# Turning the blocks behind the emptying of the sums in two pairs of a batch

## The chip, the cores and the metric

One core of a Trainium2 chip runs the whole kernel. The metric is the device time of one execution in microseconds (us); less is better. The engines are named PE (matrix multiplies, with its weight loads shown apart as PEld), DVE (VectorE), ACT (ScalarE), POOL (GpSimd) and SP (which here issues the transfers).

## What is computed

The input `x` has 8 batches of 512 tokens of width 128, and two layers are applied to it. Each has an attention-like part and a feed-forward part, each on a layer-normalised input and added back to `x`. The part around the change is the first layer's attention, with 16 channels of width 64:

```python
qz_u = qz @ ternary_factor_u.T * SCALE      # [8, 512, 16 * 64]
qz_v = qz @ ternary_factor_v.T * SCALE
message_F = einsum('bcsr,bctr->bcst', qz_u, qz_v)
qh = sigmoid(message_F)
qh_v1 = einsum('bcst,bctr->bcsr', qh, qz_v)
qh_v2 = einsum('bcst,bcsr->bctr', qh, qz_u)
message_G = (qh_v1 @ ternary_factor_u + qh_v2 @ ternary_factor_v) * SCALE
```

The other parts are a mixture of 8 experts with top-64 choice (first layer), a linear attention with a hierarchical low-rank state, evaluated by running sums over tokens, and a gated feed-forward (second layer).

## The kernel before

Each engine has its own instruction stream, in an order written out by hand, and semaphores tie the streams together. After a head of some 160 us (normalisation, routing, experts, the first pair of channels), an iteration of the main part does the first layer's attention of batch i, and between its steps the second layer (`l1`) of batch i - 1. There are 8 such iterations: the first, `iteration(0, True, False)`, has no second layer in it, the other seven do; a tail does the last second layer.

Two channels are a pair, of which a batch has 8 (j from 0 to 7). A pair takes two halves of an iteration (h from 0 to 15, j = h // 2, o = h % 2), one for each of the two products `qh_v1` and `qh_v2`. On PE a half is: 4 units of scores (`scores`, each 6 products of 64 rows, three for each channel of the pair); what stands for that half in the table `MIDDLE` (the next pair's projections "pu" and "pv", the output projection "pj", steps of the second layer); then the 4 weighted sums of tokens (`weighted`, 16 matmul records) into one bank, bank 4 for o = 0 and bank 6 for o = 1. ACT turns the scores of each unit into tanh (the sigmoid in another form), L1203. A unit of `weighted` needs the tanh of its own unit and of the third unit at least.

DVE in a half does the steps of `MIDDLE` that are its own, and then `evac_o`: it empties the bank of the sums into `o_hl`, a high part (L874) and a low part (L876), when PE has finished the half's fourth weighted sum. PE's fourth unit of scores of the following half writes the same bank, so `scores` waits there, at `u % TB == 3`, for `s_oe`, which the low part raises.

In the first half of each pair (o = 0) DVE also does `turn`: it transposes the raw projections of the next pair, `raw`, in blocks of 32 by 32 into `blocks` (L799). SP waits for `s_turned` and issues 16 transfers that put the blocks in order into `tok` (`move_tokens`, L553), each with 32 KB. The first `weighted` of the next pair, two halves later, waits until all 16 have landed (`s_moved`), and so does the next `turn`, which writes `blocks` again. ACT writes the next raw projections into `raw` (L1148) after `turn` has raised `s_turned`.

The other DVE lines that are spoken of are L925 (`TENSOR_TENSOR_SCAN`, the running sum of a step "A"), L923 and L931 (the products of steps "A" and of "C" and "D"), L866 (`add_g`, the sum of the output projection) and L904 (the step "back"). On ACT, L1035 copies a step "B".

All matmuls go through one helper or another and so stand at a few lines; they are told apart by their operands. `psum<-v_parts,u_parts` are scores with o = 0 and `psum<-u_parts,v_parts` scores with o = 1. A `psum<-arena` of 128*64 is a weighted sum.

Of the kernel before, what the change touches and what calls it, by code (L numbers as in the profile page):

```python
# [117 lines left out]
PREP_K = {"pu": 1, "pv": 2}  # L118

QUARTERS = 4  # L120
MOVED = 16 * QUARTERS * QUARTERS


# [13 lines left out]
def steps_of(work):  # L137
    return work[1] if work[0] == "rows" else (work,)
# [58 lines left out]
def is_prep(work):  # L197
    return work[0] in ("pu", "pv", "pj", "sc")


def prep_index(g, k):


    return 3 + k if is_first(g) else g * 2 + 5 + k


def moved_count(i, j):

    return (i + (j > 0)) * MOVED

# [5 lines left out]
def build(nc, io):  # L216
    ctx = ExitStack()
    with ctx:
# [14 lines left out]
        def x_bank(work, second=True):  # L233
            return bank[(X_BANK if second else FIRST_X_BANK)[work]]
# [256 lines left out]
        def _(sp):  # L491
# [56 lines left out]
            def move_tokens(i, j):  # L548

                sp.wait_ge(s_turned, i * PAIRS + j)  # L550
                for r in range(QUARTERS):
                    for a in range(QUARTERS):
                        sp.dma_start(tok[32 * r:32 * r + 32, (j + 1) % 2, :, :, 32 * a:32 * a + 32].rearrange("t w k c -> t (w k) c"),  # L553
                                     blocks[32 * a:32 * a + 32].rearrange("t w (k r c) -> t (w k) r c", k=TB, r=QUARTERS)[:, :, r])\
                          .then_inc(s_moved[j], 16)
# [77 lines left out]
        def _(dve):  # L633
# [151 lines left out]
            def prep_u(g, q, par):  # L785
                dve.wait_ge(s_prep_free, prep_index(g, 1) + 1)
                if q is not None:
                    dve.wait_ge(s_f, (q - 1) * 16)
                split(u_raw, u_hl, par).then_inc(s_us, 1)

            def prep_v(g, par):
                dve.wait_ge(s_prep_free, prep_index(g, 2) + 1)
                split(v_raw, v_hl, par).then_inc(s_vs_rdy, 1)

            def turn(i, j):

                if not (isinstance(i, int) and i == 0 and j == 1):
                    dve.wait_ge(s_moved[(j - 1) % PAIRS], moved_count(i if j else i - 1, (j - 1) % PAIRS))
                nc.vector.transpose(blocks[:].rearrange("p w t -> p (w t)"), raw.rearrange("p w t -> p (w t)")).then_inc(s_turned, 1)  # L799

            def split_rows(batch):

                link(nc.vector.tensor_copy(xn1_hl[:, 0], xn1T[:, batch]))
                nc.vector.tensor_tensor(xn1_hl[:, 1], xn1T[:, batch], xn1_hl[:, 0], ALU.subtract).then_inc(s_x1, 1)
# [50 lines left out]
            def add_g(i, j):  # L855

                bk = x_bank(("pj", j), not (isinstance(i, int) and i == 0))
                dve.wait_ge(s_pj_full, i * PAIRS + j)
                if isinstance(i, int) and i == 0 and j == 2:
                    dve.wait_ge(s_pj_free, 1)  # L860
                    before = g0
                else:
                    before = gT[:]
                if isinstance(i, int) and i == 0 and j == 3:
                    dve.wait_ge(s_scf, 1)
                nc.vector.scalar_tensor_tensor(gT[:], bk[:], 0.5 * FACTOR_SCALE ** 2, before, ALU.mult, ALU.add).then_inc(s_pj_free, 1)  # L866

            def evac_o(g, j, o, some_before):

                total = sums[:, o, j % 2:j % 2 + 1]  # L870
                dve.wait_ge(s_out, g * 8 + 4 * (o + 1))
                if some_before:
                    dve.wait_ge(s_pj_full, g)
                nc.vector.tensor_scalar(o_hl[:, o, 0], o_bank[o][:], total, None, ALU.add).then_inc(s_oh, 1)  # L874
                dve.wait_ge(s_oh, g * 2 + o + 1)
                nc.vector.scalar_tensor_tensor(o_hl[:, o, 1], o_bank[o][:], total, o_hl[:, o, 0], ALU.add, ALU.subtract)\  # L876
                  .then_inc(s_oe, 1)

            def add_y(r, L):

                bk = x_bank(("y", r))
                dve.wait_ge(s_y, L * ROUNDS + r + 1)
                if r == 0:
                    ins = nc.vector.tensor_copy(y_sb[:], bk[:])
                else:
                    dve.wait_ge(s_yadd, L * ROUNDS + r)
                    ins = nc.vector.tensor_tensor(y_sb[:], bk[:], y_sb[:], ALU.add)
                ins.then_inc(s_yadd, 1)

            def l1_statistics(L):  # L890
                wait_emptied(dve, ("back", 0), L)
                link(variances(L, mv_s))
                nc.vector.tensor_scalar(ve[:], mv_s[:, :, 1], EPS, None, ALU.add).then_inc(s_stats2, 1)

            def l1_rows(L):
                dve.wait_ge(s_rstd2, L + 1)
                normalised(xn_s, L, mv_s[:, :, 0:1], rstd_s[:].unsqueeze(2)).then_inc(s_xn2, 1)
# [59 lines left out]
            def scatter_operands(i):  # L957

                dve.wait_ge(s_yl, i * 16 + 16)
                link(nc.vector.tensor_tensor(y_weighted, y_rows[:], pick_value[:, i].unsqueeze(2).broadcast_to([P, E // 2, D]), ALU.mult))  # L960
                link(nc.vector.tensor_copy(y_hl[0][:], kf32[:]))
                for e2 in range(E // 2):
                    nc.vector.tensor_scalar(selT[e2], tokens[:], pick_at[:, i, e2:e2 + 1], None, ALU.is_equal)
                nc.vector.tensor_tensor(y_hl[1][:], kf32[:], y_hl[0][:], ALU.subtract).then_inc(s_yp, 1)

            def start_g(i):
                dve.wait_ge(s_scat, i + 1)
                if isinstance(i, int):
                    dve.wait_ge(s_pj_free, 2)
                    nc.vector.memset(g0, 0.0).then_inc(s_ones, 1)  # L970
                    nc.vector.tensor_tensor(gT[:], scatter_bank(i)[:], gT[:], ALU.add).then_inc(s_scf, 1)
                else:
                    nc.vector.tensor_copy(gT[:], scatter_bank(i)[:]).then_inc(s_scf, 1)
# [5 lines left out]
            def iteration(i, attn, second):  # L979
                if not attn:  # L980
                    add_g(i, 0)
                    for step in L1_STEPS:
                        l1(step, i - 1, last_banks[STEP_AT[step] % len(last_banks)])
                        if step == ("back", 0):
                            l1_statistics(i - 1)
                            l1_rows(i - 1)
                    return
                for h in range(0 if second else FIRST_HALF, HALVES):
                    j, o = h // 2, h % 2
                    g = i * PAIRS + j  # L990
                    some_before = second or j > 1
                    if h == (0 if second else FIRST_SCATTER_HALF - 1):
                        scatter_operands(i)
                    for work in MIDDLE[h] if second else FIRST_MIDDLE[h]:
                        if work[0] == "sc":
                            start_g(i)
                        elif work[0] == "pu":
                            prep_u(g, g + 1 if some_before else None, (j + 1) % 2)
                        elif work[0] == "pv":
                            prep_v(g, (j + 1) % 2)  # L1000
                        elif work[0] == "pj":
                            add_g(i, j)
                        elif not is_prep(work) and second:
                            for step in steps_of(work):
                                l1(step, i - 1, x_bank(step))
                    if h == HALVES - 3:
                        dve.wait_ge(s_prep_full, prep_index(g, 2) + 1)
                        dve.wait_ge(s_ones, 2)
                        split_rows(i + 1)
                    if second and h == L1_AT["back", 0]:  # L1010
                        l1_statistics(i - 1)
                        l1_rows(i - 1)
                    if o == 0:
                        if not some_before:
                            for n in range(2):
                                dve.wait_ge(s_ymv[n], 16 * E)
                        turn(i, j)
                    evac_o(g, j, o, some_before)
                    for r in range(ROUNDS):
                        if second and Y_AT[r] == h:  # L1020
                            add_y(r, i - 1)

            iteration(0, True, False)

            def body(i):
# [790 lines left out]
```

## Time and profile before

| | |
|---|---|
| median of 3 runs | 1441.76 us (1440.23 to 1442.63) |
| the profiled execution, its own time | 1442.26 us |
| its span, first to last instruction | 1440.1 us |
| PE busy | 1379.7 us, 96% of the span |
| DVE busy | 897.1 us, 62% |
| ACT busy | 697.7 us, 48% |
| the core's granted TensorE clock, mean | 0.990 |
| blocks turned (L799) | 63 times, 1.23 us each |

The span is what the trace covers; some 2.2 us of the execution's time lie around it. Busy shares are averages over the whole span. Where an engine waits, the timeline and the list of waits show it beside the instruction that came after: `[0.78 <-DVE o_hl L876]` says that the engine stood idle for 0.78 us until the DVE instruction of line 876 that writes `o_hl` released it.

### The profile page before, as it was taken

To read this page: it belongs to the slowest core of one execution; us is meant where nothing else is said; L and a number is where in the kernel's file an instruction comes from. 1 tells how busy PE (TensorE), PEld (TensorE's weight loads), DVE (VectorE), ACT (ScalarE), POOL (GpSimd) and SP (SyncE) were. 2 spreads that over 40 slices of the span, in tenths; PEclk is the share of its full clock that TensorE was granted. 3 is DMA by queue.
4 is the path that set the end of the run, shared out by engine and by line. 5 is a ranking of instruction groups with operands and counts; after the bars stand their busy time and mean duration, and the time that the engine had idled before them with its cause. 6 is when DMAs were issued, how large, how long until landed. Compare 5 with 4: busy or idle time off the path is not lost.

```text
span 1440.1 us, 24389 instructions
## 1 busy us (share of the span) xinstructions
PE 1379.7 (96%) x7814; PEld 788.6 (55%) x7814; DVE 897.1 (62%) x1546; ACT 697.7 (48%) x1077; POOL 44.7 (3%) x41
## 2 busy tenths in 40 slices
PE   5989899999999999999999999999999999999977
PEld 3556554455565555555655556555555555555544
DVE  7868544556656566566556565665655665656657
ACT  6556554454444553454535545445445444454431
POOL 4000400000000000000000000000000000000000
PEclk9999999999999999999999999999999999999988
DMA  6012122222112221111222112211122211222110
GB/s 211 1 31 68 37 37 30 30 38 31 26 26 35 36 31 29 33 32 29 30 31 35 32 26 30 39 33 28 24 37 38 30 26 24 35 30 30 27 26 8
DMA packets 298256, 50.66 MB, mean 35 GB/s; under 512 B 276192, under 2 KB 296416, under 8 KB 298112
## 3 DMA queue, kind: packets, MB, share of 16 engines
q1 hardware_dynamic: 297776, 47.29, 19.4%
q8 instruction: 67, 1.10, 0.3%
q0 software_dynamic: 336, 1.64, 0.3%
q14 instruction: 77, 0.63, 0.2%
HBM read 11.64 MB, written 4.19 MB: 11 GB/s over the span
## 4 chain that ended last, share of the span: by engine, by line
issue 85%; PE 2%; DVE 1%; POOL 1%; ACT 0%; POOLq 0%; DVEq 0%
PE psum L1264 2%; DVE arena L925 0%; POOL v_w_hl L614 0%; POOL u_w_hl L614 0%; DVE arena L923 0%; DVE arena L931 0%; POOL rstd_s L629 0%; ACT arena L1035 0%; PE psum L1626 0%; DVE xn_s L669 0%; POOL u_w_hl L611 0%; POOL v_w_hl L611 0%; POOL up_hl L614 0%; DVE x_all L940 0%; POOL gate_hl L611 0%
## 5 line engine op out<-in xcount | busy, mean ns | idle before, releaser
L1203 ACT ACTIVATE arena<-psum 128x1024 f32<-128x1024 f32 x504 | 477.0, 1031 | 611.0 <-PE psum L1264 604.0
L1264 PE MATMUL psum<-arena 128*64 128x512 f32 x2016 | 462.2, 601 | 4.8 <-ACT arena L1203 4.8
L1264 PEld LDWEIGHTS psum<-arena 128*64 128x64 f32 x2016 | 133.9, 137 | 264.8 <-issue 244.3
L1264 PE MATMUL psum<-v_parts,u_parts 64*128 64x512 f32 (+1 forms) x1568 | 208.3, 402 | 12.8 <-DVE o_hl L876 12.6
L1264 PE MATMUL psum<-u_parts,v_parts 64*128 64x512 f32 x1536 | 196.3, 399 | 4.0 <-issue 3.3
L1264 PEld LDWEIGHTS psum<-v_parts,u_parts 64*128 64x128 f32 (+1 forms) x1568 | 144.1, 185 | 101.3 <-issue 58.3
L1264 PEld LDWEIGHTS psum<-u_parts,v_parts 64*128 64x128 f32 x1536 | 139.8, 184 | 84.1 <-issue 39.9
L874 DVE TENSOR_SCALAR o_hl<-psum,sums 128x512 fp32r<-128x512 f32 x126 | 93.5, 742 | 83.3 <-PE psum L1264 82.2
L876 DVE SCALAR_TENSOR_TENSOR o_hl<-psum,sums,o_hl 128x512 fp32r<-128x512 f32 x126 | 94.6, 751 | 4.5
L931 DVE TENSOR_TENSOR arena<-psum,arena 128x512 f32<-128x512 f32 x96 | 64.5, 689 | 50.4 <-PE psum L1264 48.4
L1148 ACT ACTIVATE arena<-psum 128x512 f32<-128x512 f32 x128 | 77.3, 628 | 18.3 <-PE psum L1264 18.3
L782 DVE CAST u_parts<-arena 128x512 fp32r<-128x512 f32 x64 | 28.3, 443 | 83.4 <-ACT arena L1148 83.4
L799 DVE STREAM_TRANSPOSE blocks<-arena 128x1024 f32<-128x1024 f32 x63 | 77.7, 1234 | 0.0
L923 DVE TENSOR_TENSOR arena<-psum,arena 128x512 f32<-128x512 f32 x32 | 22.1, 691 | 80.7 <-PE psum L1264 53.7
L925 DVE TENSOR_TENSOR_SCAN arena<-ones,arena 128x512 f32<-128x512 f32 x56 | 68.6, 1224 | 1.9
L1264 PE MATMUL psum<-sel_r,uT_hl 128*128 128x512 f32 x189 | 60.1, 426 | 0.0
L1264 PE MATMUL psum<-o_hl,u_w_hl 128*128 128x512 f32 x189 | 54.0, 394 | 1.7 <-DVE o_hl L876 1.7
L1264 PE MATMUL psum<-sel_r,vT_hl 128*128 128x512 f32 x189 | 54.4, 396 | 0.0
L1264 PE MATMUL psum<-o_hl,v_w_hl 128*128 128x512 f32 x189 | 53.2, 390 | 0.0
L1264 PE MATMUL psum<-arena,top_w 128*64 128x512 f32 x96 | 50.5, 608 | 1.5 <-DVE arena L931 1.5
L1264 PE MATMUL psum<-arena,bot_w 128*64 128x512 f32 x96 | 50.5, 608 | 0.0
L783 DVE TENSOR_TENSOR u_parts<-arena,u_parts 128x512 fp32r<-128x512 f32 x64 | 48.4, 756 | 2.2
(214 smaller groups left out, 1515.2 us busy)
## 6 DMA issues: line engine op xcount, KB each, us to landing
arena<-blocks SPq DMA_DIRECT2D x1008, 32.0 KB, 2.0
x_all<-in_x SPq DMA_DIRECT2D x4, 512.0 KB, 6.1
upper<-in_we SPq DMA_DIRECT2D x8, 256.0 KB, 2.7
expert_rows<-upper SPq DMA_DIRECT2D x16, 128.0 KB, 2.5
xn_s<-expert_rows SPq DMA_DIRECT2D x8, 256.0 KB, 2.9
out<-x_all SPq DMA_DIRECT2D x8, 256.0 KB, 2.8
arena<-in_e POOLq DMA_DIRECT2D x1, 896.0 KB, 6.5
arena<-in_wi POOLq DMA_DIRECT2D x1, 576.0 KB, 6.7
```

Of the source, the lines that this page charges most:

```text
L782: link(nc.vector.tensor_copy(hl[:, par, 0], raw[:]))
L783: return nc.vector.tensor_tensor(hl[:, par, 1], raw[:], hl[:, par, 0], ALU.subtract)
L799: nc.vector.transpose(blocks[:].rearrange("p w t -> p (w t)"), raw.rearrange("p w t -> p (w t)")).then_inc(s_turned, 1)
L874: nc.vector.tensor_scalar(o_hl[:, o, 0], o_bank[o][:], total, None, ALU.add).then_inc(s_oh, 1)
L876: nc.vector.scalar_tensor_tensor(o_hl[:, o, 1], o_bank[o][:], total, o_hl[:, o, 0], ALU.add, ALU.subtract)\
L923: nc.vector.tensor_tensor(ab[:], bk[:], bs_of(f)[:], ALU.mult).then_inc(s_ld, 1)
L925: link(nc.vector.tensor_tensor_scan(pre[:], ones[:], ab[:], 0.0, ALU.mult, ALU.add))
L931: nc.vector.tensor_tensor(pc[half][:, r % 2], bk[:], pre[:], ALU.mult).then_inc(s_ld, 1)
L1148: nc.scalar.activation(raw[:], bk[:], ACT.Copy, accum_out=total[:, par:par + 1]).then_inc(s_prep_free, 1)
L1203: nc.scalar.activation(th_of(un), psum[:, at:at + 2], ACT.Tanh, scale=0.5 * FACTOR_SCALE ** 2).then_inc(s_th, 2)
L1264: return nc.tensor.matmul(out, lhsT, rhs, start=start, stop=stop)
```

## The change

In the iterations that carry the second layer, for j = 0 and j = 2 (the first and the third pair, so h = 0 and h = 4), DVE does `evac_o` first and `turn` after it. For the other six pairs, and in the whole first iteration, `turn` stays in front. So of the 63 turns 14 are moved. No instruction is added or taken away.

```diff
+LATE_TURNS = (0, 2)
...
-                    if o == 0:
+                    late = second and j in LATE_TURNS
+                    if o == 0 and not late:
                         if not some_before:
                             for n in range(2):
                                 dve.wait_ge(s_ymv[n], 16 * E)
                         turn(i, j)
                     evac_o(g, j, o, some_before)
+                    if o == 0 and late:
+                        turn(i, j)
```

## Rows read from the trace of the kernel before

**Rows 1.** The page's first part: engine, busy us, share of the span, instructions.

```profile
PE 1379.7 (96%) x7814; PEld 788.6 (55%) x7814; DVE 897.1 (62%) x1546; ACT 697.7 (48%) x1077; POOL 44.7 (3%) x41
```

**Rows 2.** The waits: engine, line, releaser; us in total, times, the longest.

```profile
PE psum L1264 <- DVE o_hl L876: 14.3, 13, 3.5
```

**Rows 3.** Timeline of DVE, third pair: start us, us, engine, line, what.

```profile
644.55 1.23 DVE L799 STREAM_TRANSPOSE blocks<-arena 128x1024 f32<-128x1024 f32 x1
645.71 0.71 DVE L874 TENSOR_SCALAR o_hl<-psum,sums 128x512 fp32r<-128x512 f32 x1
646.46 0.75 DVE L876 SCALAR_TENSOR_TENSOR o_hl<-psum,sums,o_hl 128x512 fp32r<-128x512 f32 x1
650.04 0.69 DVE L923 TENSOR_TENSOR arena<-psum,bs_more 128x512 f32<-128x512 f32 x1 [2.83 <-ACT bs_more L1035]
...
652.02 0.69 DVE L931 TENSOR_TENSOR arena<-psum,arena 128x512 f32<-128x512 f32 x1
652.84 0.75 DVE L874 TENSOR_SCALAR o_hl<-psum,sums 128x512 fp32r<-128x512 f32 x1
```

**Rows 4.** Timeline of PE over the same stretch and the pair after it.

```profile
640.63 3.65 PE L1264 MATMUL psum<-arena 128*64 128x512 f32 x16
644.22 2.34 PE L1264 MATMUL psum<-v_parts,u_parts 64*128 64x512 f32 x18
647.34 0.96 PE L1264 MATMUL psum<-v_parts,u_parts 64*128 64x512 f32 x6 [0.78 <-DVE o_hl L876]
...
649.14 3.65 PE L1264 MATMUL psum<-arena 128*64 128x512 f32 x16
...
660.77 3.65 PE L1264 MATMUL psum<-arena 128*64 128x512 f32 x16
```

**Rows 5.** Timeline of ACT over the same stretch.

```profile
645.38 2.86 ACT L1203 ACTIVATE arena<-psum 128x1024 f32<-128x1024 f32 x3 [5.03 <-PE psum L1264]
648.49 1.02 ACT L1203 ACTIVATE arena<-psum 128x1024 f32<-128x1024 f32 x1 [0.26 <-PE psum L1264]
649.41 0.59 ACT L1035 ACTIVATE bs_more<-psum 128x512 f32<-128x512 f32 x1
```

**Rows 6.** First pair of batch 2, DVE and PE.

```profile
445.88 1.23 DVE L799 STREAM_TRANSPOSE blocks<-arena 128x1024 f32<-128x1024 f32 x1
447.03 0.71 DVE L874 TENSOR_SCALAR o_hl<-psum,sums 128x512 fp32r<-128x512 f32 x1
...
445.03 2.63 PE L1264 MATMUL psum<-v_parts,u_parts 64*128 64x512 f32 x18
448.58 0.98 PE L1264 MATMUL psum<-v_parts,u_parts 64*128 64x512 f32 x6 [0.92 <-DVE o_hl L876]
```

**Rows 7.** First pair of batches 4 (762, 763) and 6 (1080).

```profile
762.83 1.23 DVE L799 STREAM_TRANSPOSE blocks<-arena 128x1024 f32<-128x1024 f32 x1
764.07 0.75 DVE L874 TENSOR_SCALAR o_hl<-psum,sums 128x512 fp32r<-128x512 f32 x1
...
763.95 3.02 PE L1264 MATMUL psum<-v_parts,u_parts 64*128 64x512 f32 x24
...
1080.49 1.23 DVE L799 STREAM_TRANSPOSE blocks<-arena 128x1024 f32<-128x1024 f32 x1
...
1080.77 3.40 PE L1264 MATMUL psum<-v_parts,u_parts 64*128 64x512 f32 x24
```

**Rows 8.** DVE after the first pair's emptying, batch 3.

```profile
609.14 0.69 DVE L904 TENSOR_TENSOR x_all<-psum,x_all 128x512 f32 x1 [2.12 <-PE psum L1623]
```

**Rows 9.** The moves: SP's issues (third pair, batches 3 and 1), time to landing, PE's need.

```profile
645.82 10.43 SPq L553 DMA_DIRECT2D arena<-blocks  x16
...
328.88 11.54 SPq L553 DMA_DIRECT2D arena<-blocks  x16
...
DMA to landing us min/median/max: 1.9/2.0/3.5
...
343.74 1.51 PE L1264 MATMUL psum<-arena 128*64 128x512 f32 x6
```

## The prediction

> **What bounds the kernel now.** I began with the busy shares: PE is at work for 1379.7 of 1440.1 us [rows 1], so outside the head the time is PE's, and a change to DVE's order counts only where PE stands still for DVE. The list of waits has such an entry: PE waited for the low part of the emptied sums (L876) 13 times, 14.3 us in all [rows 2]. That is the wait for `s_oe` at a half's fourth unit of scores. I then went through PE's timeline for these 13. One is in the first iteration (3.50 us, of which the change takes nothing), one in the tail (1.73 us, the same). The other eleven are all in the two pairs that the change touches: seven in the third pair, one for each iteration with a second layer, 0.71 to 0.79 us each (5.4 together), and four in the first pair, 0.91 or 0.92 us each (3.7 together), in batches 2, 3, 5 and 7. A third pair looks like this. PE's weighted sums start at 640.63 and last 3.65, to 644.28; its next scores follow without a gap at 644.22, eighteen products, three units; the fourth unit starts only at 647.34 [rows 4]. On DVE `turn` starts at 644.55, when the sums are already complete, and the emptying follows at 645.71 and ends at 646.46 + 0.75 = 647.21 [rows 3]. DVE has no idle time in between. So the fourth unit is 0.13 us behind the end of the emptying, and 1.16 us of the wait's cause are the turn.
>
> How much PE loses I take from the length of a whole block of 24 score products: undisturbed 3.02 us [rows 7]; in the third pair 647.34 + 0.96 - 644.22 = 4.08 [rows 4], in the first pair of batch 2 448.58 + 0.98 - 445.03 = 4.53 [rows 6], in that of batch 6 3.40 [rows 7]. That is 1.06, 1.51 and 0.38 us too long. The idle figures in brackets are smaller, because they count from the modelled end of the last product.
>
> **Part 1, the emptying moved forward, third pair.** In its new place it can start at 644.55 instead of 645.71 (645.71 - 644.55 = 1.16 earlier), ends near 646.05, and an undisturbed fourth unit would start about 647.34 - 1.06 = 646.3. The wait is gone, and 1.06 us are on offer. PE can't take all of it. The half's weighted sums (649.14) need the tanh of the third unit, and ACT does three of them back to back from 645.38, to 648.24 [rows 5]; these units are scored ahead of the wait and come no earlier. 649.14 - 648.24 leaves 0.90. Behind the sums DVE is the next to be late: its product of step A (650.04) waits for ACT's copy of step B (649.41), which follows the fourth tanh (648.49, 0.26 us of idle time ahead of it) [rows 3, 5]. This chain can move up by some 0.26 to 0.30 only, and it ends in the product at 652.02, 0.69 long, right in front of the half's own emptying at 652.84. With PE 0.9 earlier that emptying would come some 0.55 us after PE's sums. In an undisturbed pair the emptying (0.75 + 0.75 behind a start 0.05 after the sums) ends 3.02 - 0.96 - 1.5 = about 0.5 us ahead of the unit that waits for it, so this lateness is just hidden. I take 0.8 us for each: 7 x 0.8 = 5.6. The bounds are 0.3, if the ACT chain sets the pace, and 1.06.
>
> **Part 2, the emptying moved forward, first pair.** In batch 2 DVE starts `turn` at 445.88, the emptying at 447.03 [rows 6]; that is 1.15 us, and the block was 1.51 too long, so all 1.15 are returned. DVE comes late by itself there (its work at the head of an iteration), so 0.36 us of the wait stay. The other three look alike: 4 x 1.15 = 4.6. In batch 6 the turn starts at 1080.49, before the sums end; the block is 0.38 too long, and I take 0.25 to 0.38, say 0.3. In batch 4 the sums' emptying starts at 764.07, on time with the turn at 762.83 in front of it [rows 7], and batch 1 is like it: nothing to gain. Together 4.9. What follows is not short of ACT here: the transposes, and eight products of the scatter lie between the scores and the weighted sums. What DVE is late with depends on how the iterations' boundaries fall; between none and all six of the iterations 2 to 7 late by the full turn, the bounds are 0 and 6 x 1.15 = 6.9.
>
> **Part 3, the turn moved back.** DVE's time is the same, 1.23 us in either place. Behind it stands DVE's next work: in the third pair L923, ahead of which DVE idles 2.83 us [rows 3], in the first pair L904, ahead of which it idles 2.12 [rows 8]. Either hides the 1.16 us that the turn now takes there: after the gain the turn ends at about 647.2 against L923 at 649.7. Without that cover it would be 1.2 us for each of 14, 17 us.
>
> The turn's end starts the 16 transfers. In a third pair it moves from 645.78 to about 647.2, by 1.45 (the length of the emptying, less their overlap). SP issues the 16 in 10.43 us, from 645.82 to 656.25; the last is issued some 0.65 before that and lands 2.0 later, at 657.6. The weighted sums that need it start at 660.77 [rows 4, 9]: 3.2 us of slack. It shrinks by 1.45 and by the 0.8 that PE comes earlier, to 0.9. In batch 1 SP takes 11.54 us from 328.88 on, the landing is at 341.8, the need at 343.74 [rows 9]: 1.95 - 2.25 = -0.3, so that one loses 0.3. In the first pairs the slack before was 2.4 to 3.9 by the same reckoning; the turn moves by 1.45 where DVE was late and by 2.7 (764.07 + 1.5 against 762.83) where it was not, and 0 to 1.2 us are left. I take 0.3 for pair three of batch 1 and nothing else. The bounds: nothing at all, or, if SP needs 11.54 everywhere, 0.3 more in each of about ten, 3 us.
>
> Here a rule speaks against the change. The landing takes 2.0 us from issue, in every place [rows 9], and the gap between landing and need is what the later turn uses up. The Trainium skill, "DMA: Bandwidth & Descriptors", Rules for kernel authors, says to issue a DMA early and wait on its semaphore late, so that its fixed setup cost overlaps; the change issues 14 x 16 of them later. By that rule alone the sum would be a loss where the slack is used up; the rows say that it is not quite.
>
> **Sum.** 5.6 + 4.9 - 0.3 = 10.2 us, against the profiled execution's own 1442.26: 1432.1. The median of the runs shown is 0.5 below that execution, so I put the median of the new kernel at 1431.7.
>
> **Rivals.**
> - *Only the first pairs pay.* In the third pair, ACT's fourth tanh and DVE's products hold the pace, and each yields 0.3: 4.9 + 2.1 - 0.3 = 6.7, so 1435. For it speaks that ACT has only 0.26 us idle there; against it, that DVE's own lateness is covered by 0.5 us. Chance 0.13.
> - *No change.* The time that PE wins is given back before the iteration ends, at its boundary or at steps whose releaser does not move. Speaks for it: PE waits for ACT in many small places. Against: the waits with a fixed time are none; each chain starts from PE's own products. 1441.8, give or take 1. Chance 0.07.
> - *The moves come late.* This is the one on the other side. If the 16 transfers need longer when issued later, PE's weighted sums of the second and fourth pair wait. The gain is 10.5 over 14 places, 0.75 us for each, so it decides when the mean wait passes 0.75, that is when landing comes some 1.5 us later than reckoned. With the longest landing seen (3.5 against 2.0) and the slower issue (11.54 against 10.43) it is 2.6 later, less 0.9 of slack, 1.7 for each: 14 x 1.7 - 10.5 = 13 us slower, 1455. Both are rare in the trace. Chance 0.04.
> - *The first pairs are late by another pattern.* With none late the gain is 5.3 (1436.5), with six late 5.3 + 6.9 = 12.2 (1429.5). This is part of the forecast's own range.
>
> **Numbers.** The forecast has a chance of 0.76, with 1429.5 to 1434.5 as its own range. With the rival of the first pairs, the range is 1429 to 1436.5. A difference below 0.2% (2.9 us) can hardly be told from no change here. Faster by more than that: 0.88; within it: 0.08; slower: 0.04.
>
> **What would show it.** The waits of PE for L876 fall from 13 to some 6, and from 14.3 to about 6.5 us: the two outside, and the rest of 0.3 us in the late first pairs. A third pair's scores block is about 3.0 to 3.2 us long instead of 4.08. In the first and third pair L799 stands behind L876. The first `weighted` of the second and fourth pair shows no wait for the moves but in batch 1. The forecast is wrong if PE's gap reappears in front of weighted sums, if DVE's L874 in the half after the third pair is late by more than 0.5 us, or if the first pairs' lateness is gone or everywhere.

## The result and the profile after

The changed kernel takes 1432.2 us in the median of 4 runs (1431.69 to 1434.59), the kernel before 1441.91 us beside it. The ratio is 0.9938 with a 95% interval from 0.9922 to 0.9954: faster by 0.6%, 9.7 us, against a forecast of 1431.7. Two later measurements of the same kernel gave 1435.25 and 1435.73 us (below), 6.2 and 6.5 us less than before by their ratios; the first ratio makes it 8.9. So the gain is somewhere from 6 to 9 us, and the 0.5 us between forecast and first result say little. The profiled execution is the slowest of the 4: 1434.59 us, its span 1432.6.

The page's first part and three rows of the waits, after:

```profile
PE 1374.9 (96%) x7814; PEld 787.8 (55%) x7814; DVE 897.0 (63%) x1546; ACT 696.6 (49%) x1077; POOL 44.7 (3%) x41
```

```profile
PEld psum L1270 <- DVE o_hl L879: 7.5, 11, 4.0
PE psum L1270 <- DVE o_hl L879: 5.2, 2, 3.5
PEld psum L1270 <- DMA arena<-blocks: 4.8, 7, 1.1
```

L1270, L879, L877, L802 and L926 are the L1264, L876, L874, L799 and L923 of before; L1209 and L1041 on ACT are its L1203 and L1035. PE's wait for the emptied sums went from 14.3 us, 13 times [rows 2] to 5.2 us, twice: only the two outside the change are left. The weight loads (PEld) still wait for L879 eleven times. The longest, 4.0 us, is the one in the first iteration; the others are of 0.22 or 0.45 us and cost PE little: in the first pairs of batches 3, 5 and 7 the block of 24 score products takes 3.29 to 3.33 us, where an undisturbed one takes 3.02. A wait that was not there has come instead: seven times for the moved blocks.

The third pair of batch 3, DVE and PE (start, us; compare [rows 3, 4]):

```profile
642.54 0.74 DVE L877 TENSOR_SCALAR o_hl<-psum,sums 128x512 fp32r<-128x512 f32 x1
643.31 0.75 DVE L879 SCALAR_TENSOR_TENSOR o_hl<-psum,sums,o_hl 128x512 fp32r<-128x512 f32 x1
643.98 1.23 DVE L802 STREAM_TRANSPOSE blocks<-arena 128x1024 f32<-128x1024 f32 x1
647.65 0.69 DVE L926 TENSOR_TENSOR arena<-psum,bs_more 128x512 f32<-128x512 f32 x1 [2.44 <-ACT bs_more L1041]
```

```profile
638.62 3.65 PE L1270 MATMUL psum<-arena 128*64 128x512 f32 x16
...
642.20 3.04 PE L1270 MATMUL psum<-v_parts,u_parts 64*128 64x512 f32 x24
...
646.27 3.65 PE L1270 MATMUL psum<-arena 128*64 128x512 f32 x16
...
656.43 0.86 PE L1270 MATMUL psum<-o_hl,u_w_hl 128*128 128x512 f32 x3
657.12 0.84 PE L1270 MATMUL psum<-o_hl,v_w_hl 128*128 128x512 f32 x3
658.14 3.65 PE L1270 MATMUL psum<-arena 128*64 128x512 f32 x16 [0.17 <-DMA arena<-blocks]
```

The 24 score products are one unbroken block of 3.04 us (4.08 before). From one start of weighted sums to the next it is 646.27 - 638.62 = 7.65 us, where it was 649.14 - 640.63 = 8.51: 0.86 gained. From there to the fourth pair's sums it is 658.14 - 646.27 = 11.87, where it was 660.77 - 649.14 = 11.63: 0.24 given back, at the wait for the blocks.

These intervals, taken for all halves of all seven batches from the starts of PE's weighted sums, are the account that the rest goes by (us, sum over the seven batches, against the profiled execution of before):

| kernel | first pair, half 0 to 1 | half 1 to 2 | third pair, half 4 to 5 | half 5 to 6 |
|---|---|---|---|---|
| the change | -4.50 | 0.00 | -5.91 | +2.44 |
| the change, second measurement | -3.75 | +0.26 | -5.93 | +3.66 |
| the change, third measurement | -4.66 | +0.04 | -5.92 | +2.71 |

All other halves together differ by less than 0.3 us, but for the step from one iteration to the next (+0.5 in the first two rows, +2.4 in the third, of which 2.26 us in one batch). The stretches that the change does not touch differ as well: the head and the first iteration together by +1.0, -1.6 and 0.0 us in the three rows, the time after the last half by -1.0, -1.3 and -1.3. So a difference of 1 or 2 us between two whole times says nothing about a half, and the halves are compared one by one.

What held up the blocks? SP issues them as before, in 10.43 us, and a usual landing would be 1.4 us after the end of that, at 657.1:

```profile
645.24 10.43 SPq L556 DMA_DIRECT2D arena<-blocks  x16
```

PE, and so the blocks, were ready only at 658.14. The transfers by queue, in the stretch from 655.7 to 658.1 us (packets, MB, share of the 16 DMA engines):

```profile
q1 hardware_dynamic: 529, 0.06, 20.6%
q8 instruction: 1, 0.02, 2.4%
```

One packet loads instructions. Its share of 2.4% of 16 engines over 2.4 us is 0.92 us on one of them: the reading is that it stands in front of the last blocks' packets there. (The trace does not name the engine of a packet, so this much is inferred, from a landing that comes 1.0 us late.) The Trainium skill, "Runtime: NRT & Kernel Launch", Instruction fetch mechanics, says that an engine's sequencer fetches its instructions ahead by DMA, 256 at a time in blocks of 16 KiB, and that this is mostly hidden. The trace agrees with the size (0.02 MB). In the kernel before, the stretch from 656.3 to the landing at 657.6 shows queue q1 alone:

```profile
q1 hardware_dynamic: 516, 0.06, 36.2%
```

There the load came later, behind the landing. In the trace after such a packet meets the end of the third pair's moves in six of seven batches, all but batch 1, and these six are the ones that lose: 0.23 to 0.77 us each, batch 1 only 0.03.

### The profile page after: what moved, and what is told of

It reads as the page before. It is cut to its first block, busy times and chain, and to the rows that moved or that the text cites. A ratio compares the mean times of both kernels' runs of the same rounds, so it can differ in the third digit from the quotient of the medians.

```text
span 1432.6 us, 24389 instructions
## 1 busy us (share of the span) xinstructions
PE 1374.9 (96%) x7814; PEld 787.8 (55%) x7814; DVE 897.0 (63%) x1546; ACT 696.6 (49%) x1077; POOL 44.7 (3%) x41
## 4 chain that ended last, share of the span: by engine, by line
issue 86%; DVE 2%; POOL 1%; PE 1%; ACT 0%; POOLq 0%; DVEq 0%
PE psum L1270 1%; DVE arena L928 1%; DVE arena L926 0%; DVE arena L934 0%; POOL v_w_hl L617 0%; POOL u_w_hl L617 0%; POOL rstd_s L632 0%; DVE arena L950 0%; ACT arena L1041 0%; PE psum L1632 0%; DVE xn_s L672 0%; POOL u_w_hl L614 0%; POOL v_w_hl L614 0%; POOL up_hl L617 0%; DVE x_all L943 0%
## 5 line engine op out<-in xcount | busy, mean ns | idle before, releaser
L1209 ACT ACTIVATE arena<-psum 128x1024 f32<-128x1024 f32 x504 | 475.7, 1031 | 604.7 <-PE psum L1270 597.8
L1270 PE MATMUL psum<-arena 128*64 128x512 f32 x2016 | 462.4, 601 | 7.6 <-ACT arena L1209 4.8
L1270 PEld LDWEIGHTS psum<-arena 128*64 128x64 f32 x2016 | 134.0, 137 | 268.5 <-issue 241.3
L1270 PE MATMUL psum<-v_parts,u_parts 64*128 64x512 f32 (+1 forms) x1568 | 205.0, 401 | 4.2 <-DVE o_hl L879 3.5
L1270 PE MATMUL psum<-u_parts,v_parts 64*128 64x512 f32 x1536 | 196.4, 399 | 4.6 <-issue 3.9
L1270 PEld LDWEIGHTS psum<-v_parts,u_parts 64*128 64x128 f32 (+1 forms) x1568 | 145.0, 185 | 88.6 <-issue 51.1
L1270 PEld LDWEIGHTS psum<-u_parts,v_parts 64*128 64x128 f32 x1536 | 139.3, 184 | 85.2 <-issue 45.3
L877 DVE TENSOR_SCALAR o_hl<-psum,sums 128x512 fp32r<-128x512 f32 x126 | 93.8, 745 | 88.4 <-PE psum L1270 88.2
L879 DVE SCALAR_TENSOR_TENSOR o_hl<-psum,sums,o_hl 128x512 fp32r<-128x512 f32 x126 | 94.6, 751 | 4.4
L802 DVE STREAM_TRANSPOSE blocks<-arena 128x1024 f32<-128x1024 f32 x63 | 77.7, 1234 | 0.0
L926 DVE TENSOR_TENSOR arena<-psum,arena 128x512 f32<-128x512 f32 x32 | 22.1, 690 | 80.2 <-PE psum L1270 53.4
L1270 PE MATMUL psum<-sel_r,uT_hl 128*128 128x512 f32 x189 | 60.1, 426 | 0.0
L1270 PE MATMUL psum<-o_hl,u_w_hl 128*128 128x512 f32 x189 | 54.0, 394 | 1.7 <-DVE o_hl L879 1.7
L1270 PE MATMUL psum<-sel_r,vT_hl 128*128 128x512 f32 x189 | 54.5, 396 | 0.0
L1270 PE MATMUL psum<-o_hl,v_w_hl 128*128 128x512 f32 x189 | 53.2, 390 | 0.0
L1270 PE MATMUL psum<-arena,top_w 128*64 128x512 f32 x96 | 49.3, 595 | 1.5 <-DVE arena L934 1.5
L1270 PE MATMUL psum<-arena,bot_w 128*64 128x512 f32 x96 | 49.3, 595 | 0.0
```

Source lines behind the costliest of these rows:

```text
L926: nc.vector.tensor_tensor(ab[:], bk[:], bs_of(f)[:], ALU.mult).then_inc(s_ld, 1)
L1209: nc.scalar.activation(th_of(un), psum[:, at:at + 2], ACT.Tanh, scale=0.5 * FACTOR_SCALE ** 2).then_inc(s_th, 2)
L1270: return nc.tensor.matmul(out, lhsT, rhs, start=start, stop=stop)
```

## The experiments

**The changed kernel again, and three edits of it.** The three were made to tell two readings of the new wait apart: the load of instructions (theory 1), or blocks that are simply too late (theory 2).

> The changed kernel itself, beside the three others of this call. All theories: 1432 us, 0.993 of the kernel before. Its trace should again show PE waiting for the moved blocks in front of the weighted sums of the fourth pair (half 6) in all seven batches, 0.2 to 0.7 us each, some 2.4 us in all.

1435.25 us (1434.4 to 1435.87, 5 runs), ratio 0.9957 [0.9944, 0.9971]. The wait is there in all seven batches, but it costs more, 3.66 us. The time expected was missed by 3 us. The two profiled executions are alike in time, 1434.40 us for this one and 1434.59 for the first, but not in their parts. The wait for the blocks is 1.2 us longer in this one and the first pairs gain 0.75 less; against that, 3.0 us less are spent where the change does nothing: 1.6 in the head, 1.0 in the first iteration and 0.4 after the last half.

> The changed kernel with 32 small products in PE's stream at its very beginning, where PE waits for the first rows anyway. They compute nothing that is used; they shift all later instructions of PE by some 128. Theory 1 (instruction loads at fixed places of PE's stream meet the last moves of the third pair): the loads fall some 10 us elsewhere, the landing of the third pair's moves comes 1.4 us after SP's last issue instead of 2.4, the waits ahead of half 6 go: 2 us less, about 1430 us, unless the loads now meet the moves of the first pair. Theory 2 (simply too late): nothing changes, 1432 us.

```diff
             pe.wait_ge(s_first, 16 * len(first_consts))
+            for _ in range(32):
+                mm(bank[7][:, 0:4], ident[:], ident[:, 0:4])
```

1440.68 us (11 runs), ratio 0.9991 [0.9982, 1.0]. The products were not free: they waited for a load and then took 13.8 us, which made the head some 7 us longer. Behind the head the expectation of theory 1 holds: half 5 to 6 costs 0.56 us instead of 2.44 to 3.66. Of these, 0.41 are in batch 1, where a load of instructions now meets the end of the moves, and the six batches that it has left lose at most 0.07 each: the loss goes where the packet goes.

> The changed kernel with 8 of the third pair's 16 moves issued by POOL, the other 8 by SP, in the seven late batches; POOL waits for the turn as SP does. Both theories: the moves land 2 us or more earlier if POOL issues one in under 1 us, the waits ahead of half 6 go, and the third pair keeps all of its 0.86 us: 2.4 us less, about 1429.8 us. If POOL needs much more than 1 us for each, it is slower than the changed kernel: 8 x 1.5 = 12 us from the turn on would land after the need and cost some 0.5 us in each batch.

```diff
+            with pool.Fori(0, B - 1) as n:
+                rstd_rows(n)
+                pool.wait_ge(s_turned, n * PAIRS + PAIRS + 2)
+                pool.tensor_tensor(pool_idle[:], powc[:], powc[:], ALU.add)
+                for r in range(QUARTERS // 2, QUARTERS):
+                    for a in range(QUARTERS):
+                        move_block(pool, 2, r, a, s_moved_pool)
+            rstd_rows(B - 1)
...
-                for r in range(QUARTERS):
+                for r in range(QUARTERS // 2 if j == 2 and not (isinstance(i, int) and i == 0) else QUARTERS):
```

1430.68 us (1429.33 to 1431.45), ratio 0.9922 [0.9908, 0.9936]: 4.6 us less than the changed kernel beside it, where 2.4 was expected. POOL and SP issue side by side (batch 3):

```profile
644.27 4.66 POOL L503 DMA_DIRECT2D arena<-blocks  x8
```

```profile
644.08 5.20 SPq L503 DMA_DIRECT2D arena<-blocks  x8
```

Both are done 5 us sooner, so that one packet of 0.92 us can't hold them up until the need, and half 5 to 6 is back at -0.06 us. It keeps the whole gain of the third pair and gives nothing back. Not all of the 4.6 us are the moves: 2.4 to 3.7 are the wait for them, and another 1.3 us stand in the halves from 6 on, in each batch alike. Those the kernel with two queues and all turns in front has too (below), and what they come from is not shown.

> The changed kernel with add_g (L869, 0.68 us) of the first and third pair put behind the turn: DVE empties the sums, turns, adds. The turn, and with it the 16 moves, ends about 0.6 us earlier where DVE was late. Theory 1 (the last transfers of the third pair stand behind a transfer of 16 KB that loads instructions, which comes at a place of PE's stream): the moves that meet it land when it is done, so the waits of the fourth pair stay, and only the 0.3 us that is left of the wait for the sums in the late first pairs comes back, four times: 1431 us. Theory 2 (the moves are simply too late by 0.2 to 0.7 us, because they begin 1.45 us later): the waits go, 2.4 + 1.2 us less, 1428.5 us.

```diff
-                            add_g(i, j)
+                            if not (second and j in LATE_TURNS):
+                                add_g(i, j)
...
                     if o == 0 and late:
                         turn(i, j)
+                        add_g(i, j)
```

1477.95 us (1476.16 to 1480.79), ratio 1.0257 [1.0243, 1.0271]. Neither theory had this. PE, in the first pair of batch 3, and the waits:

```profile
613.58 0.96 PE L1272 MATMUL psum<-v_parts,u_parts 64*128 64x512 f32 x6
617.04 3.70 PE L1272 MATMUL psum<-v_parts,u_parts 64*128 64x512 f32 x18 [2.50 <-DVE arena L869]
```

```profile
PEld psum L1272 <- DVE arena L869: 36.0, 14, 3.0
```

`add_g` empties a bank too. In the first pair it is bank 2, and the next half's second unit of scores writes it, two units sooner than the bank of the sums is written; in the third pair it is bank 6, which the third unit writes, one unit sooner. Put behind the emptying and the turn it makes the seven first pairs 24.6 us longer than in the kernel before and the third ones 13.4, by the same account. Only part of that is PE standing still, 30.0 us in 14 waits against some 48 us that the two pairs lose to the changed kernel. Much of the rest is the clock: behind the stand of 2.50 us above, the granted clock is 0.57 in the mean from 617.04 to 620.50, near its lower level (1.2 GHz), and 18 score products take 3.70 us instead of 2.34 [rows 4]. The trace has 11 stretches at the lower level in the seven batches, 41 us in all; the changed kernel's trace has none there. The run says nothing about the theories. But the changed kernel has this wait once: in batch 2 of its first profile PE stands 0.64 us for L869, since DVE is late as a whole there, and that first pair gains 0.53 instead of 1.15 us.

**One pair at a time, and the shift again, hidden.**

> Only the first pair's turn is put behind the emptying (LATE_TURNS = (0,)). By the account of the changed kernel's trace the first pairs give 4.5 us and lose next to nothing to late moves: 1437.3 us against 1441.8. If the gain of the first pairs depended on the third, it would be nearer to 1441.

> Only the third pair's turn is put behind the emptying (LATE_TURNS = (2,)). By the account it gains 0.86 us seven times, 5.9 us, gives 2.4 to 3.6 us back in front of the fourth pair's weighted sums, where the moves land late, and wins 0.2 elsewhere: 1438.2 to 1439.4 us. The sum of this gain and of that of the other run should be the whole gain, 6.5 to 9.7 us. If the moves did not cost anything, it would be 1435.9.

`LATE_TURNS = (0,)`: 1435.36 us, ratio 0.9965 [0.9952, 0.9979], 6.0 us less than before. `LATE_TURNS = (2,)`: 1438.14 us, ratio 0.9974 [0.9964, 0.9985], 3.2 us less. Their accounts are those of the change, each for its own pair: -4.73 in the first pairs and nothing in half 4 to 6; -5.92 in the third pairs and +2.87 behind them, -0.09 in the first. The parts add up (6.0 + 3.2 = 9.2, where the whole gave 6 to 9), and half by half one does not depend on the other; the times alone are too coarse to show it (the nine runs of the second spread over 6.3 us). So the third pair's turn, which takes more off PE's wait, earns less.

> The changed kernel with 22 small products of ones in PE's stream at its very beginning, ahead of the loads, where PE waits 11 us for the first rows; nothing reads their result. They shift PE's later instructions by some 88. Theory 1 (a load of instructions at fixed places of PE's stream meets the last moves of the third pair): the loads come some 7 us earlier in each half 5, the last moves land 1.4 us after SP's last issue, the waits ahead of half 6 shrink from 0.2 to 0.9 us each to 0.1 or less: 2.4 to 3.5 us less than the changed kernel on the same chip (1432 to 1435), so 1429.5 to 1432. Theory 2 (the moves are too late by themselves): no change.

```diff
+            pe.wait_ge(s_ones, 1)
+            for _ in range(22):
+                mm(bank[7][:, 0:4], ones[:, 0:P], ones[:, 0:4])
             pe.wait_ge(s_first, 16 * len(first_consts))
```

1431.6 us (1430.51 to 1434.23), ratio 0.9936 [0.9923, 0.995]. Half 5 to 6 costs 0.10 us instead of 2.44 to 3.66, with the turn exactly as late as in the change. Batch 3, SP's issues, PE, and the transfers from 653.9 to 655.6 us:

```profile
643.06 10.81 SPq L556 DMA_DIRECT2D arena<-blocks  x16
```

```profile
644.08 1.51 PE L1270 MATMUL psum<-arena 128*64 128x512 f32 x6
...
655.71 3.65 PE L1270 MATMUL psum<-arena 128*64 128x512 f32 x16
```

```profile
q1 hardware_dynamic: 535, 0.06, 28.5%
```

655.71 - 644.08 = 11.63, as before the change, and there is no load of instructions at the moves' end. In the wider stretch from 645 to 653 us there is one, in the middle of the moves. This settles it for theory 1: a load at the end of the moves makes the wait, and a turn that is equally late without it does not. The late turn is the other half of the cause, for it uses the slack up. In batches 2, 4 and 5 of this run the blocks land only 0.04 to 0.08 us ahead of the weighted sums, and in the kernel before a load met the end of batch 4's moves without any loss, since 2.5 us of slack were left there. The whole time says less than the account: by the ratios this run gains 0.3 us more than the change in its first measurement, and 2.7 to 3.0 more than in the later two.

The packet did not vanish, it moved, and it costs something in its new place too. In the third pairs of batches 2 to 7 it falls among the issues, and SP takes 10.8 to 11.3 us for the 16 instead of 10.4; batch 1, which has none, is at 10.4. In two first pairs (batches 1 and 7) half 1 to 2 now takes 0.56 and 0.35 us more.

> The kernel before, all turns in front, with the third pair's moves shared between SP and POOL as in the run of two queues (1430.7 us with the late turns). If the shared queue only takes away the wait that the late turn made, it gives nothing here, where the moves have 2 to 3 us of slack: 1441.8, within 0.7. If it helps by itself (less traffic, freer SP), it would be 1 us or more faster.

1440.82 us (11 runs), ratio 0.9995 [0.9986, 1.0004]. Half 5 to 6 differs by 0.1 us from the kernel before: a second queue takes no wait away where the moves have slack. The halves from 6 on are 1.3 us shorter in the profiled execution, as they are with the late turns; in the time only 0.05% can be seen, at most 0.14%.

**The limits.**

> The changed kernel once more, as the measure for the others of this call. It had 1432.2 and 1435.3 us so far; so between these.

1435.73 us (1435.23 to 1436.48), ratio 0.9955 [0.9942, 0.9969]: 0.4 us above the upper end of what was expected.

> The turn behind the emptying in all eight pairs of the seven batches. In the six others the emptying was on time with the turn in front, so there is nothing to gain, and the turn begins 1.5 to 2.8 us later; their moves had 2.1 to 5.9 us of slack. Theory 1 (moves cost only where they land after the need, and a load of instructions adds up to 1.5 us to a landing): pairs with h = 6, 12 and 14 come near the limit; 1 to 3 us slower than the changed kernel. Rival (a late turn costs nothing as long as DVE has idle time behind it): the same as the changed kernel.

`LATE_TURNS = tuple(range(PAIRS))`: 1452.74 us (1449.93 to 1453.15), ratio 1.0069 [1.0056, 1.0083], 17 us slower than the changed kernel. Both expectations are wrong by far. The account shows, against the changed kernel, the same loss, 0.5 to 0.6 us, in every batch at halves 6, 8, 10, 12 and 14 (3.8, 3.6, 3.7, 3.7 and 3.4 us, 18.2 in all), and 0.5 us at half 13, of which 0.36 us in batch 3, where PE waits for the blocks. The first pairs gain 1.3 us more than in the change. DVE and PE at half 6 of batch 3:

```profile
668.52 0.75 DVE L879 SCALAR_TENSOR_TENSOR o_hl<-psum,sums,o_hl 128x512 fp32r<-128x512 f32 x1
669.19 1.24 DVE L802 STREAM_TRANSPOSE blocks<-arena 128x1024 f32<-128x1024 f32 x1
670.35 0.65 DVE L887 COPY arena<-psum 128x512 f32<-128x512 f32 x1
```

```profile
671.06 0.96 PE L1270 MATMUL psum<-v_parts,u_parts 64*128 64x512 f32 x6 [0.24 <-DVE arena L887]
```

From half 6 on `add_y` (L887, L890) follows the emptying on DVE, and it too frees a bank for the next half's fourth unit. A turn between them is in front of a bank that PE wants. The first three pairs have no `add_y` behind the turn; pair two lost nothing by its late turn (half 2 to 3: 0.01 us).

> The changed kernel with the moves of the first and the third pair shared between SP and POOL, 8 each. Against the sharing in the third pair alone (1430.7 us) it takes away what the first pairs' moves still cost when a load of instructions meets them, 0.1 to 0.9 us in the traces so far: 1430.2 us, at most 1 us better.

1430.64 us (1429.1 to 1432.23), ratio 0.9919 [0.9905, 0.9933]: no better than sharing the third pair's moves alone. Half 1 to 2 takes 1.43 us more than in the kernel before: about 0.3 in batches 2, 3, 5 and 7, and 0.16 in batch 1. The trace shows why. POOL has work of its own there, the `rstd_s` of the second layer. In batch 3 it is issuing the first pair's moves from 603.32 to 607.92 and starts `rstd_s` only at 607.93, 0.37 us after its input is ready; DVE waits 1.44 us for the result instead of 1.15, empties the half's sums that much later, and PE waits 0.33 us for them.

> The kernel before with the same 22 small products at the beginning of PE's stream. Its moves have slack, so where the loads of instructions fall should not matter: 1441.5 us, within 0.7. If shifting PE's stream helped by itself, by other means than the moves, it would be faster by 2 to 3 us.

1442.83 us (11 runs), ratio 1.0001 [0.9992, 1.001]: the shift alone is worth nothing.

## Why the prediction was right, and where it was not

- **What bounds the kernel**: right. The eleven waits of 9.1 us in the two pairs are gone from PE's list, which has 2 entries and 5.2 us where some 6 and 6.5 were forecast; the rest of 0.3 us in the late first pairs is there, in blocks of 3.3 us instead of 3.02.
- **Part 1, 0.8 us for a third pair**: 0.84 to 0.86 in six batches, 0.79 in the first, 5.91 in all against 5.6. ACT's chain holds as it was read: its four tanh now run without a gap (3.77 us from 643.36 on), and the product of step A is 647.65 - 646.27 = 1.38 us behind the start of the weighted sums instead of 650.04 - 649.14 = 0.90. This lateness stays hidden, as was reckoned; no wait for L879 appears in the next half.
- **Part 2, 4.9 us for the first pairs**: 4.50 in the first profile, 3.75, 4.66, 4.73 and 4.47 in others. Four batches late, one by a part, two not: the same pattern. In the first profile the deficit is batch 2 alone, which gains 0.53 instead of 1.15 since PE then waits for `add_g`; in the two later ones waits of 0.12 to 0.70 us for `add_g` stand in some of the late batches. The forecast had DVE late by itself there, but not this wait: DVE is late as a whole, and moving the turn does nothing for the step ahead of it.
- **Part 3, the cover behind the turn**: right. DVE still waits 2.44 us ahead of L926 with the turn in front of it.
- **Part 3, the landing of the moves, 0.3 us**: the term that was mis-sized, and its place was wrong. It is 2.44 us, and 2.7 and 3.7 in the other two measurements. The forecast put 0.3 in batch 1 and nothing elsewhere; batch 1 lost 0.03 (SP took 11.10 us there and not 11.54), the six others 0.23 to 0.77 each. The prediction had named a gap of PE in front of weighted sums as a sign that it is wrong, and this sign came. The slack of 0.9 us was worked out well (the landing would have been at 657.1, the need at 657.9), but with 2.0 us as the landing time "in every place", which is the median of a row that goes up to 3.5. The trace of before showed what can go wrong: in batch 4 the blocks landed 2.6 us after the last issue, with a load of instructions in the stretch. The bound given, 3 us, has about the right size and came from SP's 11.54 us in batch 1. There a load of instructions falls among the issues (at 331.5), as in the shifted kernel above, so it was the same packet by its other effect. The rival with late moves had its mechanism right; its mean wait is 2.44 / 7 = 0.35 us in the third pairs and nearly nothing in the first, below the 0.75 at which it decides.
- **The slack in the first pairs, 0 to 1.2 us**: right. The blocks land 0.1 to 1.1 us ahead of the need.
- **The rule on early issue**, from the Trainium skill ("DMA: Bandwidth & Descriptors", Rules for kernel authors), speaks to this term: the trace agrees in that the later issue cost 2.4 us, and not in the sign of the whole.
- **The sum**: 10.2 us against the own time of the profiled execution, which fell by 7.7 (1442.26 to 1434.59). Of the 2.5 between them, 2.1 are the moves, 0.1 the first and third pairs together, and the rest lies outside the changed halves. That the first median met the forecast within 0.5 us is in part luck, for the sum was 2.1 us too good in the moves: the two others are 3.6 and 4.0 above it, inside the range of 1429 to 1436.5 but outside the forecast's own, 1429.5 to 1434.5.

## What to carry to other kernels

When two operations of one engine both have somebody waiting, list for each the time of the need: here the sums' bank, the other emptied banks and the blocks, and put the earliest first. The same reordering that wins 0.9 to 1.15 us in a late place costs 0.5 us in a half where another bank's emptying stands behind it. A slack of 0.9 us on the landing of these transfers was not slack: read the latest landings, not the median, and look for what else the DMA engines carry then. If the landing has no slack, let a second queue issue half; it took the wait of 2.4 to 3.7 us away here, and was worth nothing where there was slack. But look at the work that the second engine has itself: sharing one pair more made POOL late with its own step and gave 1.4 us back.

## What the hardware showed that was not expected

- Loads of instructions (one packet of 0.02 MB each) go over the same DMA engines as the kernel's data: one of them takes 0.92 us of an engine's time. Where one comes at the end of the 16 moves, the last lands 2.6 to 3.5 us after its issue instead of 2.0 (in batch 3 at 658.1 instead of 657.1); where it comes in the middle, the landing is as usual and SP's issue takes longer, 10.81 us instead of 10.43 in batch 3.
- Where they fall depends on PE's instruction stream: 22 products without use at its beginning took the loads away from the end of the third pair's moves, and at least 2.3 us of waits with them; 0.9 came back in two first pairs.
- Twice in the trace of before and in the three of the change, PE stands for 1.2 to 1.9 us with no releaser in the profile, ahead of batches 4 and 6, where its loop over two iterations jumps back. What it waits for is not shown. In the third measurement the granted clock is 0.50 (1.2 GHz) from 1068 to 1070 us, behind such a stand of 1.93 us: the next 24 score products take 4.61 us instead of 3.06. Together with the longer stand (1.23 in the kernel before) this is the 2.26 us of that batch's step. In the first measurement PE stood 1.75 us at the same place and the clock stayed at 1.00.
- The same kernel measured three times gave 1432.2, 1435.3 and 1435.7 us, each with a spread of 1.3 to 2.9 us within its runs. The traces place part of it in the moves' wait, in the step between two iterations, in the head and after the last half; what sets these from one measurement to the next stays open. The two later ones ran on two different chips.
